# Two row-aligned neighbour tiles per row block, added by VectorE, and three listed tiles: a two-layer graph attention on one core

## The reference, cut to what matters

```python
seq = (x @ W_seq).reshape(N, H, DH)                 # 2048 x 16 heads x 32
score1 = jnp.einsum('nhd,d->hn', seq, a1)
score2 = jnp.einsum('nhd,d->hn', seq, a2)
scores = leaky_relu(score1[:, :, None] + score2[:, None, :], negative_slope=0.2)
scores = scores + (1.0 - adj)[None, :, :] * MASK_VAL
attn = softmax(scores, axis=-1)
hidden = jnp.einsum('hij,jhd->ihd', attn, seq).reshape(N, D_IN)
hidden = elu(hidden @ W_out + b_out)
x = _layernorm(x + hidden)
```

## Time and profile before

| | us |
|---|---|
| median of 3 runs (lowest, highest) | 394.93 (393.57, 396.96) |
| the profiled execution | 395.34 |
| its span, first to last instruction | 393.5 |
| TensorE busy in the span | 344.1 |
| VectorE busy | 322.2 |
| ScalarE busy | 199.8 |
| GpSimd busy | 186.6 |

### The profile page before, as it was taken

The page is one execution under the profiler, slowest core; times in us unless marked ns, Lnnn a source line. Parts: engine busy times, 40 slices in busy tenths (PEclk is TensorE's granted clock), DMA queues, the critical chain, the costliest instruction groups (busy, mean ns, idle before and its releaser), DMA issues.

```text
span 393.5 us, 5227 instructions
## 1 busy us (share of the span) xinstructions
PE 344.1 (87%) x1656; PEld 213.8 (54%) x1656; DVE 322.2 (82%) x816; ACT 199.8 (51%) x449; POOL 186.6 (47%) x178
## 2 busy tenths in 40 slices
PE   0899899999999988999999934699989999999970
PEld 0444645555444644788888813456545655665540
DVE  2999999985978477777988687778899999999772
ACT  3975874466430224555654321122446776677780
POOL 7776558777771000000000047888778878770000
PEclk9999999999999999999999975899999999999995
DMA  6999464436994402921111237665675776662014
GB/s 250 373 384 378 177 214 121 185 126 160 229 231 92 145 0 66 383 106 66 57 55 57 82 110 209 177 171 161 172 191 164 201 215 209 182 205 82 27 56 142
DMA packets 34758, 65.10 MB, mean 165 GB/s; under 512 B 15649, under 2 KB 16801, under 8 KB 32673
## 3 DMA queue, kind: packets, MB, share of 16 engines
q1 hardware_dynamic: 25632, 42.45, 32.1%
q0 software_dynamic: 9088, 22.20, 20.5%
HBM read 53.50 MB, written 8.52 MB: 158 GB/s over the span
## 4 chain that ended last, share of the span: by engine, by line
PE 41%; DVE 26%; POOL 13%; issue 7%; ACT 6%; DMA 5%; SPq 0%; DVEq 0%; ACTq 0%; POOLq 0%
PE ps L639 17%; PE ps L841 15%; POOL adjT L607 9%; DVE adjT L2006 8%; POOL pr L530 5%; DMA arenaA<-in_x_dram 2%; DVE arenaC L1878 2%; DVE adjT L1876 2%; DVE ps L1936 2%; DVE arenaA L1942 2%; DVE ps L1929 2%; PE ps L621 2%; PE ps L830 2%; DVE arenaB L1845 2%; ACT adjT L1015 1%
## 5 line engine op out<-in xcount | busy, mean ns | idle before, releaser
L639 PE MATMUL ps<-arenaB,adjT 128*128 128x512 f16 x512 | 115.6, 379 | 2.7 <-ACT adjT L1015 1.6
L530 POOL DMA_INDIRECT pr<-in_adj_dram,aidx x79 | 82.0, 1038 | 30.6 <-issue 23.0
L607 POOL DMA_INDIRECT adjT<-seqtab,eidx x64 | 77.2, 1206 | 19.5 <-issue 19.5
L955 PE MATMUL ps<-adjT,arenaB 128*128 128x264 f32 x256 | 67.9, 412 | 18.5 <-DVE adjT L2006 14.1
L639 PEld LDWEIGHTS ps<-arenaB,adjT 128*128 128x128 f16 x512 | 48.8, 98 | 59.9 <-ACT adjT L1015 3.2
L607 POOL DMA_INDIRECT adjT<-seqtab,near x16 | 21.5, 1341 | 107.6 <-DMA seqtab<-arenaA 102.9
L955 PEld LDWEIGHTS ps<-adjT,arenaB 128*128 128x128 f32 x256 | 49.4, 200 | 41.1 <-DVE ps L1936 21.1
L841 PE MATMUL ps<-stage 128*128 128x272 f32 x256 | 61.5, 394 | 0.1
L868 PE MATMUL ps<-adjT 128*128 128x512 f32 x120 | 54.1, 593 | 1.0 <-ACT ps L1135 1.0
L841 PEld LDWEIGHTS ps<-stage 128*128 128x128 f32 x256 | 47.4, 190 | 9.5 <-ACT stage L1104 0.8
L2006 DVE TENSOR_TENSOR adjT<-adjT 128x1024 f32<-128x1024 f32 (+2 forms) x35 | 47.9, 1373 | 2.3 <-ACT adjT L1231 1.9
(11 more groups left out here) (277 smaller groups left out, 486.7 us busy)
## 6 DMA issues: line engine op xcount, KB each, us to landing
stage<-in_adj_dram SPq DMA_DIRECT2D x16, 1024.0 KB, 6.1
seqtab<-arenaA SPq DMA_DIRECT2D x16, 264.0 KB, 2.0
arenaA<-in_x_dram SPq DMA_DIRECT2D x4, 1024.0 KB, 12.0
out_dram<-arenaC SPq DMA_DIRECT2D x16, 256.0 KB, 3.5
arenaB<-in_x_dram SPq DMA_DIRECT2D x1, 1536.0 KB, 10.6
pr<-in_adj_dram,aidx POOLq DMA_INDIRECT x79
arenaC<-in_L_gnn_Wq_dram SPq DMA_DIRECT2D x1, 1024.0 KB, 16.6
arenaC<-in_L_gnn_Wk_dram SPq DMA_DIRECT2D x1, 1024.0 KB, 20.0
```

The source lines that it names most:

```text
L530: g.indirect_dma_start(out=avals[:, t:t + 1], out_offset=None, in_=adj_flat, in_offset=bass.IndirectOffsetOnAxis(ap=aidx[:, t:t + 1], axis ...
L607: g.indirect_dma_start(out=Grow[:, b % GR, k, :], out_offset=None, in_=seqtab, in_offset=bass.IndirectOffsetOnAxis(ap=source, axis=0)).the ...
L639: ins = t.matmul(bank(4 + b % 2), adjT[:, b, j, :], xsplit[:, w, j, :], start=(j == 0 and w == 0), stop=(j == NB - 1 and w == 1))
L955: ins = t.matmul(bank(2 * (b % 2) + c, HALF), ehot[:, b % HOTS, k - 1, :], Grow[:, b % GR, k, c * HALF:(c + 1) * HALF], start=False, stop= ...
```

## The change

A row's two first neighbours now stay with their row, and the rest of the list is laid out over three tiles. Five tiles are fetched for each row block as before. VectorE adds both row-aligned tiles to the sums, the second after the first, between the two weighings; TensorE's matmuls start when both are added. Rows without a first or second neighbour get a weight of zero for it through `lacks`.

```diff
-    KE = 4
-    GE = KE + 1
+    KE = 3
+    NEAR = 2
+    GE = KE + NEAR
...
-                        source = near[:, b:b + 1] if k == 0 else eidx[:, b * KE + k - 1:b * KE + k]
+                        source = near[:, b, k:k + 1] if k < NEAR else eidx[:, b * KE + k - NEAR:b * KE + k - NEAR + 1]
...
-                        pe.wait_ge(e_own, b + 1)
+                        pe.wait_ge(e_own, NEAR * (b + 1))
                         pe.wait_ge(hot_made, b + 1)
-                        for k in range(1, GE):
+                        for k in range(NEAR, GE):
                             pe.wait_ge(e_mul, weighed(b, k))
                             for c in range(2):
-                                ins = t.matmul(bank(2 * (b % 2) + c, HALF), ehot[:, b % HOTS, k - 1, :],
+                                ins = t.matmul(bank(2 * (b % 2) + c, HALF), ehot[:, b % HOTS, k - NEAR, :],
...
-                v.tensor_scalar(mv[:, :, 0], mv[:, :, 1], -1.0, 0.0, ALU.add, ALU.max).then_inc(cnt_made, 1)
+                v.tensor_scalar(mv[:, :, 0], mv[:, :, 1], -float(NEAR), 0.0, ALU.add, ALU.max).then_inc(cnt_made, 1)
...
-                v.tensor_scalar(near[:], ek[:, :, 0], -1.0, 0.0, ALU.add, ALU.max)
-                v.tensor_scalar(lacks[:], deg[:, 2, :], 0.5, NONE, ALU.is_lt, ALU.mult)
+                v.tensor_scalar(near[:], ek[:, :, 0:NEAR], -1.0, 0.0, ALU.add, ALU.max)
+                for k in range(NEAR):
+                    v.tensor_scalar(lacks[:, :, k], deg[:, 2, :], k + 0.5, NONE, ALU.is_lt, ALU.mult)
...
-                v.tensor_copy(s1e[:, :, 0:H1], s1).then_inc(mxe_made, 1)
+                for k in range(NEAR):
+                    ins = v.tensor_copy(s1e[:, :, k * H1:(k + 1) * H1], s1)
+                ins.then_inc(mxe_made, 1)
...
-                    dve.wait_ge(own_laid, b + 1)
-                    dve.wait_ge(e_mul, weighed(b, 0))
-                    v.tensor_tensor(sums(b), sums(b), heads(G[:, b % GR, 0:H1]), ALU.add).then_inc(e_own, 1)
+                    for k in range(NEAR):
+                        if k == 0:
+                            dve.wait_ge(own_laid, b + 1)
+                        else:
+                            dve.wait_ge(e_own, NEAR * b + k)
+                        dve.wait_ge(e_mul, weighed(b, k))
+                        v.tensor_tensor(sums(b), sums(b), heads(G[:, b % GR, k * H1:(k + 1) * H1]), ALU.add).then_inc(e_own, 1)
...
-                            if first == 0:
+                            if first < NEAR <= last:
                                 add_nearest(b)
```

More of the change, by code:

```diff
@@ L354, in two_layer_graph_attention @@
         erow = sb("erow", [P, NB * KE])
-        near = sb("near", [P, NB], I32)
-        lacks = sb("lacks", [P, NB])
+        near = sb("near", [P, NB, NEAR], I32)
+        lacks = sb("lacks", [P, NB, NEAR])
         eidx = sb("eidx", [P, NB * KE], I32)
@@ L1827, in pick_edges @@
                         for q in range(4):
-                            ins = v.scalar_tensor_tensor(spot[:, 0, q * KE:(q + 1) * KE], rowid[:, 0:KE], 2.0,
+                            ins = v.scalar_tensor_tensor(spot[:, 0, q * KE:(q + 1) * KE], rowid[:, 0:KE], NEAR + 1.0,
                                                          sp_[:, q * KE:(q + 1) * KE, 16], ALU.add, ALU.subtract)
@@ L1839, in pick_edges @@
                     lots = sp_.rearrange("p (q k) c -> p q k c", q=4)
-                    v.tensor_tensor(s1e[:, 4 * c:4 * c + 4, H1:].rearrange("p q (k h) -> p q k h", k=KE),
+                    v.tensor_tensor(s1e[:, 4 * c:4 * c + 4, NEAR * H1:].rearrange("p q (k h) -> p q k h", k=KE),
                                     lots[:, :, :, 18:18 + H1], lots[:, :, :, 18 + H1:KW], ALU.add)
@@ L1951, in self_args @@
                     v.tensor_tensor(sa[:, 0], sa[:, 2], sa[:, 3], ALU.subtract).then_inc(self_arg, 1)
-                    v.tensor_tensor(mxe[:, :, 0:H1], sa[:, 3], lacks[:].unsqueeze(2).to_broadcast([P, NB, H1]),
-                                    ALU.add).then_inc(mxe_made, 1)
+                    for k in range(NEAR):
+                        ins = v.tensor_tensor(mxe[:, :, k * H1:(k + 1) * H1], sa[:, 3],
+                                              lacks[:, :, k:k + 1].to_broadcast([P, NB, H1]), ALU.add)
+                    ins.then_inc(mxe_made, 1)
                     dve.wait_ge(self_arg, 5)
@@ L1959, in largest @@
                     rows = "p b (k h) -> p b k h"
-                    some = mxe[:, 4 * c:4 * c + 4, H1:].rearrange(rows, k=KE)
-                    v.tensor_tensor(some, s1e[:, 4 * c:4 * c + 4, H1:].rearrange(rows, k=KE),
+                    some = mxe[:, 4 * c:4 * c + 4, NEAR * H1:].rearrange(rows, k=KE)
+                    v.tensor_tensor(some, s1e[:, 4 * c:4 * c + 4, NEAR * H1:].rearrange(rows, k=KE),
                                     M2[:].unsqueeze(1).unsqueeze(1).to_broadcast([P, 4, KE, H1]), ALU.add).then_inc(mxe_made, 1)
```

## The result

The changed kernel takes 400.56 us (median of 4; 400.21 to 402.29) against 395.28 us for the one before in the same session: ratio 1.0139, 95% interval 1.0104 to 1.0174. A second, longer session gave 1.0134 (1.0110 to 1.0157). It is slower by 1.4%, 5.3 to 5.6 us; the forecast was 1.8%, 7.2 us.

A forecast was written before the change was run, and what follows sets the result against it. VectorE's chain of waits was taken to bound the second layer from block 6 on. Terms +8.2 - 0.8 + 0.5 - 0.3 - 0.4 = +7.2 us gave 402.1 us against the median 394.93; range 398.5 to 405.0.

The forecast's parts named there:

- The bound: Second layer from block 6 on: VectorE's chain of waits sets the block, 8.02 us each; TensorE, 96% busy, follows.
- The added instruction: Second VectorE addition of 128x528 in each second-layer block: 0.82 us each, +8.2 us over blocks 6 to 15.
- The one-hots and the exponential: VectorE's one-hot comparisons narrow to 384 columns: -0.8 us in six blocks; blocks 9, 11, 13, 15 wait for ScalarE's exponential.
- The first norm: TensorE spreads three listed tiles instead of four in the first norm: -0.4 us.
- The early part: Second layer's first blocks: additions in blocks 0 to 4 covered by gather waits, +0; block 5 +0.5 us.
- the signs: What the profile should show, such as a period near 8.7 us and early gather waits about 3 us less.
- The rival of the early fetches: Blocks before 5: gathers come sooner as fewer issues are slowed, early part -3.2 us, total 398.9 us; chance 0.11.
- The end: Block 15 pays 0.82 us for its addition; behind the last weighing the tail is the same instructions, 0.
- TensorE as the bound: Second layer: TensorE sets the period, its saved 0.92 us a block makes room, so 394 us; chance 0.04.
- The clock: TensorE's clock falls after pauses in second-layer blocks, +2.3 to +4.3 us a block, about 407 us; chance 0.05.
- The fallback: A row block lists more than 384 neighbours and the dense branch runs; chance 0.01.
- The added operation and GpSimd: Second layer: VectorE's added addition doesn't slow GpSimd's gather issues; otherwise blocks 0 to 4 end 3.6 us later.

The follow-up runs named there:

- the addition alone: Kernel before with the nearest tile added twice in every block, four listed tiles and TensorE's 16 passes kept: 402.74 us, ratio 1.0185.
- tile 1 by TensorE: Changed kernel with the second row-aligned tile added by TensorE, identity as weights, instead of by VectorE: 393.66 us, ratio 0.9973 against before.
- the early additions: Kernel before with the nearest tile added twice in blocks 0 to 4 only: 394.49 us, ratio 0.9987.

## Why the prediction was right, and where its terms were off

*The bound.* Right. That the chain of waits and not the busy shares decides between two engines at 96 and 97% was the step that everything hung on, and the experiments bear it out: TensorE's 16 or 12 passes make no difference under the longer VectorE block (the addition alone), its start 0.6 us later makes none, and taking four passes away without the addition gives 0.4 us of the 9 (interval -1.1 to +0.4), all of which the narrower VectorE work can account for. Giving the four passes back (tile 1 by TensorE) costs nothing either: 71.41 us from block 6 to 15 for 72.31.

*The added instruction.* Its size was off: 0.75 us and not 0.82. I had taken the gap of 0.11 us in front of the first addition for the gap of any dependent pair. It is not: the second addition follows the first at +0.03. Over ten blocks that is 0.7 us too much. The right rows were in the trace of before, just ahead of the block of the earlier trace rows, and I did not take them: two ELU instructions, the second of which reads what the first one writes.

```profile
318.60 0.68 DVE L1876 SCALAR_TENSOR_TENSOR adjT<-ps,adjT 128x512 f32<-128x512 f32 x1
319.32 0.69 DVE L1878 SCALAR_TENSOR_TENSOR arenaC<-adjT,arenaC 128x512 f32<-128x512 f32 x1
```

318.60 + 0.68 = 319.28, and the next starts at 319.32, +0.04: by that row the addition would have been 0.72 + 0.04 = 0.76. Why the addition behind the first weighing has the longer gap is open.

*The one-hots and the exponential.* Right to a hundredth. Periods of blocks 7, 8, 12 and 14 grew by 0.61 us (0.75 - 0.14), those of 9, 11 and 13 by 0.74, since there the weighing starts with ScalarE's exponential however short the comparison is. Blocks 6 and 10, with the maxima, grew by 0.48. The nine together are +5.6 in the long stretch, 77.78 / 9 = 8.64 us each for the forecast 8.7.

*The first norm.* Right: -0.35 us forecast as -0.4, in every kernel with three listed tiles.

*The early part.* Forecast +0.5 (block 5) on top of a covered +0. Block 5 grew by 0.48 (10.18 for 9.70), but the whole stretch by about -0.2 (mean 56.8 for 57.0): block 5 began some 0.6 us sooner after the first gather. VectorE's waits for gathers fell from 6.6 us to between 2.5 and 2.9 in the three profiles, where the signs named about 3 less. The rival of the early fetches was a real mechanism, working at a fifth of its full size of -3.2. That a part of it was "as likely as the reverse" was a fair price: the additions between the weighings brought 1.06 to 1.10 us a gather, the same addition behind them 1.20. That it fell to the good side was luck, since nothing in the prediction worked out where the issues would begin.

*The end.* From the start of block 15 to the end of its second weighing 6.50 us for 5.75 in every profile of the two kernels, +0.75, forecast +0.8. Behind that weighing 27.42, 27.42 and 27.86 us for 27.80 and 27.39: the tail has the length that it had, within 0.5 us.

Sum by stages: -0.35 - 0.2 + 5.6 + 0.75 = +5.8 us, and 5.3 to 5.6 by the times, for the forecast 7.2. Of the 1.4 us between the sum and the forecast, 0.7 is the price of the addition in blocks 6 to 15 and 0.7 the early part (of it 0.07 the price again, in block 5). The range held all of it, and the mechanism was the one forecast.

*The rivals.* TensorE as the bound: refuted. Its sum was also added up wrongly: 10 x (0.82 - 0.92) - 0.4 - 0.8 is -2.2 and not about -1, so the rival stood for 392.7 us rather than 394, with the same sign. The clock: it did fall, in two stretches of one profile out of three, which the prediction had named as a sign against itself, and the price of 2.3 to 4.3 us a block did not come. The step that failed in this rival was to compare TensorE's slowed work with the block and not with the slack to the next one that needs it: the sums of a block are wanted by VectorE a whole block later, and the refilled buffer two later. The fallback did not occur.

*The added operation and GpSimd.* Right as far as it shows. An issue of 0.94 us at 302.08 lies across the end of two additions that began at 301.06; the one that began under the weighing took 1.67. The Trainium skill ("SBUF — State Buffer", "Who interferes with whom") draws the same line, between two inputs in SBUF and one.

## What to carry to other kernels

When two engines are 96 and 97% busy, work taken from the one that waits buys nothing and work given to the other costs its full start-to-start time, here 0.75 us a block; the list of waits tells which is which. Where a change has a useful half (here the shorter lists, with a row-aligned tile that needs no one-hot) and a costly half (who adds it), try the halves apart: the tile added by TensorE was 1.1 us faster than before, added by VectorE 5.3 slower. For effects under 1% compare stages of the profile between marks that scatter little, rather than whole times.

## What the hardware showed that I had not expected

An addition of 128x528 from and to PSUM that waits for the one before it starts 0.75 us after it, an instruction that waits for nothing 0.62 us, so waiting for a neighbour on the same engine costs 0.13 us. The wait here is by a semaphore, and no run has the one without the other. Reordering recovers it: 1.2 us over nine blocks.

A gather's issue on GpSimd that begins while a weighing runs, whose inputs are both in SBUF, ends 0.80 to 0.94 us after the weighing's end and so takes up to 2.18 us in the kernel before (2.43 at most in the fourteen profiles), while one that begins even 0.01 us ahead of it takes 0.94 (256.02 and 256.03 us with the early additions). So more VectorE work in the first blocks did not lengthen them, and the place of an addition in the block moved them by 0.7 us.

TensorE fell to its lower clock after pauses of 2.71 and 2.51 us in one profile of the changed kernel, and after the same two pauses stayed at 1.00 in two others. The falls had no cost: 77.78 us with them, 77.81 and 77.83 without.
